# One sequence further ahead: where x is scaled, split and transposed in a mixture-of-experts MLP kernel

## What is computed

```python
h = gelu(einsum('bsh,bhi->bsi', x, Wi[expert]) + bi, approximate=False)   # 512 -> 2048
o = einsum('bsi,bih->bsh', h, Wo[expert]) + bo                            # 2048 -> 512
r = o + x
y = (r - mean(r)) * rsqrt(var(r) + 1e-12) * gamma + beta
out = rotate(y, theta, phi)    # pairs of features turned by two angles of the sequence
```

## Time and profile before

| | |
|---|---|
| time of the kernel before | 3029.11 us, median of 3 runs (3025.92 to 3030.88) |
| the profiled execution | 3023.2 us, its span from first to last instruction 3021.5 us |
| TensorE busy | 2744.7 us (91%) |
| VectorE busy | 2377.5 us (79%) |
| GpSimd busy | 1603.3 us (53%) |
| ScalarE busy | 887.4 us (29%) |

### The profile page before, as it was taken

One profiled execution on the slowest core, in us unless ns is written; L12 is line 12 of the kernel. 1 busy time (PEld: TensorE's weight loads), 2 busy tenths in 40 slices (PEclk: granted clock), 3 DMA queues, 4 the chain that ended last, 5 costly groups with the idle time before them and its releaser, 6 DMA issues.

```text
span 3021.5 us, 54615 instructions
## 1 busy us (share of the span) xinstructions
PE 2744.7 (91%) x12306; PEld 1220.8 (40%) x12307; DVE 2377.5 (79%) x5177; ACT 887.4 (29%) x1433; POOL 1603.3 (53%) x1619
## 2 busy tenths in 40 slices
PE   2888999889999989998999999999889989999998
PEld 1333444334444434433444444444334433444443
DVE  4688878877778887888877888878887788877777
ACT  4222332223332223322333222222223222233332
POOL 4879727973017974479700478706876479700000
PEclk9899999999999999999999999999999999999999
DMA  4546445655444655546544446545465546534343
GB/s 161 139 115 166 114 132 123 161 129 126 87 101 126 159 132 128 132 111 170 118 108 91 125 114 170 128 105 142 121 153 142 132 105 164 123 87 91 80 94 70
DMA packets 742560, 375.89 MB, mean 124 GB/s; under 512 B 682816, under 2 KB 682944, under 8 KB 733824
## 3 DMA queue, kind: packets, MB, share of 16 engines
q1 hardware_dynamic: 677568, 173.95, 29.9%
q0 software_dynamic: 25984, 130.29, 13.2%
q10 hardware_dynamic: 38976, 71.32, 7.3%
HBM read 174.13 MB, written 33.55 MB: 69 GB/s over the span
## 4 chain that ended last, share of the span: by engine, by line
PE 29%; DVE 29%; DMA 23%; issue 11%; DVEq 6%; ACTq 1%; POOL 1%; ACT 1%; SPq 0%; POOLq 0%
DMA xbuf<-in_x 16%; PE z_ps L825 15%; PE o_ps L841 14%; DVE h L638 7%; DMA hT<-h 5%; DVEq L195 3%; DVE xbuf L671 2%; DVE hid L627 2%; DVE x L632 2%; DVE ln L665 2%; DVE ln L667 2%; DVE xbuf L654 1%; DVE y L686 1%; DVE turned L683 1%; DMA xT<-x 1%
## 5 line engine op out<-in xcount | busy, mean ns | idle before, releaser
L825 PE MATMUL z_ps<-wi,xT 128*128 x6096 | 1449.0, 389 | 173.3 <-DMA xT<-x 119.5
L841 PE MATMUL o_ps<-wo,hT 128*128 x6144 | 1423.8, 382 | 47.7 <-DMA hT<-h 35.0
L825 PEld LDWEIGHTS z_ps<-wi,xT 128*128 128x128 f16 x6096 | 607.8, 100 | 945.7 <-issue 287.9
L841 PEld LDWEIGHTS o_ps<-wo,hT 128*128 128x128 f16 x6144 | 605.0, 98 | 791.0 <-issue 86.2
L471 ACT ACTIVATE hid<-hid 128x512 f32<-128x512 f32 x512 | 322.0, 629 | 1507.4 <-DVE hid L627 1506.2
L638 DVE SCALAR_TENSOR_TENSOR h<-hid,tok,h 128x512 f16<-128x512 f32 x512 | 494.4, 966 | 43.5 <-ACT h L479 31.0
L405 POOL TENSOR_TENSOR wi<-staged 128x512 f32<-128x512 f32 x112 | 133.8, 1195 | 650.1 <-DVE xbuf L648 639.1
L479 ACT ACTIVATE h<-hid,tok 128x512 f16<-128x512 f32 x512 | 369.6, 722 | 281.1 <-DMA hT<-h 262.0
L627 DVE SCALAR_TENSOR_TENSOR hid<-z_ps,tok,bi_all 128x512 f32<-128x512 f32 x512 | 382.2, 747 | 80.1 <-DVE y L686 28.1
L338 POOL TENSOR_SCALAR staged<-staged,wscale 128x512 f32<-128x512 f32 x224 | 197.7, 883 | 20.9
L646 DVE TENSOR_SCALAR ln<-inv,ex 128x1 f32 (+1 forms) x128 | 27.3, 214 | 211.5 <-issue 173.8
(11 more groups left out here) (124 smaller groups left out, 1771.3 us busy)
## 6 DMA issues: line engine op xcount, KB each, us to landing
staged<-in_L_cond_Wi POOLq DMA_DIRECT2D x56, 1024.0 KB, 5.7
staged<-in_L_cond_Wo POOLq DMA_DIRECT2D x56, 1024.0 KB, 6.1
xbuf<-in_x ACTq DMA_DIRECT2D x128, 256.0 KB, 2.7
out<-y ACTq DMA_DIRECT2D x128, 256.0 KB, 2.2
hT<-h SPq DMA_TRANSPOSE x512, 3.1
bi_all<-in_L_cond_bi POOLq DMA_DIRECT2D x7, 1024.0 KB, 7.5
wi<-in_L_cond_Wi SPq DMA_DIRECT2D x4, 1024.0 KB, 8.7
wo<-in_L_cond_Wo ACTq DMA_DIRECT2D x4, 1024.0 KB, 11.7
```

The source lines that it names most:

```text
L825: last = t.matmul(z_ps[:, n, :], xT16[:, j, a, k, :], wi16[:, bass.ds(b, 1), w, k, cs], start=(k == 0 and (a, w) == PASSES[0]), stop=(k == ...
L841: last = t.matmul(o_ps[:, j, :], hT16[:, n, a, c, :], wo16[:, bass.ds(b, 1), w, n * GC + c, :], start=(n == 0 and c == 0 and (a, w) == PAS ...
```

## The change

x is scaled and split one sequence further ahead. ScalarE, in iteration s, sums the squares of x(s+2) instead of x(s+1) and makes the high half of x(s+2) after the last `gelu_bank` instead of that of x(s+1) between banks 0 and 1; x is fetched three sequences ahead. The Gelu of bank 3 also waits for the transpose of x(s+1), since `x16` is overwritten next. VectorE makes the low half of x(s+1) at the head of the iteration, ahead of the residual, instead of after z bank 1, and the scale of x(s+2) after z bank 1 instead of that of x(s+1) after z bank 0. SyncE issues the transpose of x ahead of that of bank 3 of h. Before the loop, x(1) is summed, scaled and split among the boot work.

```diff
--- before.py
+++ after.py
@@ -257,10 +257,10 @@
                                        h16[:, n % HB].rearrange("p a t -> p (a t)")).then_inc(s_hT[n], 16)
 
             def iteration(s, k, inner=False):
+                if there(s, 1, inner):
+                    transpose_x(1 - k)
                 if there(s, -1, inner):
                     transpose_h(NB - 1)
-                if there(s, 1, inner):
-                    transpose_x(1 - k)
                 if there(s, 0, inner):
                     for n in range(NB - 1):
                         transpose_h(n)
@@ -465,8 +465,10 @@
                 act.sem_clear(s_sx)
                 a.activation(x16[:, 0, :], x_of(s), ACT.Copy, scale=SX).then_inc(s_xhi, 1)
 
-            def gelu_bank(s, k, n):
+            def gelu_bank(s, k, n, ahead):
                 hb = hid[:, n * BANK:(n + 1) * BANK]
+                if ahead and n == NB - 1:
+                    act.wait_ge(s_xT, (s + 2) * 16)
                 act.wait_ge(s_z, s * NB + n + 1)
                 a.activation(hb, hb, ACT.Gelu).then_inc(s_gelu, 1)
                 act.wait_ge(s_gelu, s * NB + n + 1)
@@ -484,18 +486,16 @@
                 act.dma_start(out[bass.ds(b, 1), :, :].rearrange("a t n -> t (a n)"), y[:]).then_inc(s_y, 16)
 
             def iteration(s, k, inner=False):
-                ahead, here = there(s, 1, inner), there(s, 0, inner)
-                if there(s, 2, inner):
-                    fetch_x(s + 2, k)
+                ahead, here = there(s, 2, inner), there(s, 0, inner)
+                if there(s, 3, inner):
+                    fetch_x(s + 3, 1 - k)
                 if ahead:
-                    sum_x(s + 1, 1 - k)
+                    sum_x(s + 2, k)
                 if here:
-                    gelu_bank(s, k, 0)
+                    for n in range(NB):
+                        gelu_bank(s, k, n, ahead)
                 if ahead:
-                    hi_x(s + 1)
-                if here:
-                    for n in range(1, NB):
-                        gelu_bank(s, k, n)
+                    hi_x(s + 2)
                 if there(s, -2, inner):
                     store(s - 2)
 
@@ -525,16 +525,20 @@
             e0 = slot_value(act, EXPERT, 0, E - 1)
             fetch_x(1, 1)
             sum_x(0, 0)
+            fetch_x(2, 0)
             squares(0, 1)
             hi_x(0)
             squares(0, 2)
             squares(0, 3)
+            sum_x(1, 1)
             for q in range(Q):
                 act.dma_start(by_rows(raws[1][:, q * QN:(q + 1) * QN]),
                               wo_quarter(e0, q)).then_inc(s_braw[Q + q], 16)
             act.wait_ge(s_ang, 1)
             a.activation(angle[:, 20:24], angle[:, 16:20], ACT.Sin).then_inc(s_sin, 1)
             hi_parts(0)
+            act.wait_ge(s_xT, 16)
+            hi_x(1)
             for q in range(Q):
                 squares(1, q)
             iteration(0, 0)
@@ -699,6 +703,8 @@
                     b, r = 0, 0
                 elif here:
                     b, r = slot_value(dve, BUF, s, 1), slot_value(dve, RANK, s, E - 1)
+                if ahead:
+                    lo_x(s + 1)
                 if last:
                     b2 = slot_value(dve, BUF, s - 2, 1)
                     residual(s - 2, k, b2)
@@ -709,8 +715,6 @@
                     moments(s - 2, b2)
                 if here:
                     z_bank(s, 0, b)
-                if ahead:
-                    scale_x(s + 1)
                 if back:
                     lo_group(s - 1, 1 - k, NB - 1)
                 if last:
@@ -718,8 +722,8 @@
                     normalise(s - 2, b2)
                 if here:
                     z_bank(s, 1, b)
-                if ahead:
-                    lo_x(s + 1)
+                if there(s, 2, inner):
+                    scale_x(s + 2)
                 if here:
                     lo_group(s, k, 0)
                 if last:
@@ -769,6 +773,7 @@
             v.tensor_scalar(angle[:, 16:18], r, -1.0, 1.5707963267948966, ALU.mult, ALU.add).then_inc(s_ang, 1)
 
             total(0)
+            scale_x(1)
```

## The result

The changed kernel takes 3132.52 us (median of 4 runs, 3131.84 to 3134.12) against 3027.52 us of the kernel before on the same chip (4 runs, 3025.89 to 3030.88): **105 us slower, ratio 1.0346, 95% interval 1.0328 to 1.0364.** The forecast was 3127 us.

What follows compares the result with a forecast made beforehand. The prediction took VectorE to bound most iterations. Its terms, 11 + 55 + 93 - 23 - 30 - 8 = +98 us on a profiled 3023.2 us, gave 3121; the runs' median is 5.9 us higher, hence 3127 us, range 3023 to 3190.

Steps and rivals of the forecast that it cites:

- VectorE sets the pace: Steady state: VectorE bounds 105 of 123 iterations, so removing TensorE's 119.5 us of waits gains nothing by itself.
- first stretch: Timeline from 725 to 894 us, GpSimd idle: eight iterations, 768 matmuls, 169 us, TensorE setting the pace.
- second stretch: Timeline from 1528 to 1697 us, GpSimd idle: eight iterations, 169 us, VectorE setting the pace.
- The low half of x at the head: VectorE's head: waits about 1 us for ScalarE's high half, with the third register load standing behind that wait.
- Rival 2: VectorE's head: the third load covers the low half if the high half ends 0.9 us sooner; 2937 us, chance 0.07.
- The stall in the quiet iteration: VectorE's head, GpSimd idle and VectorE pacing: 0.4 us in each of 27 iterations, +11 us.
- TensorE-paced iterations: 18 iterations where TensorE sets the pace: VectorE's 0.98 us wait for bank 3 covers the delay, 0 us.
- Late transposes: 19 iterations where bank 1's transpose of h lands late: the mean delay at VectorE's head is 4.9 us, +93 us.
- GpSimd busy: VectorE's head in 59 iterations with GpSimd working: mean delay 0.9 us, +55 us.
- Credits: VectorE's waits for TensorE shrink, -30 us; the middle of its list sheds a slowed low half, -8; boot 0.
- The scale of x behind z bank 1: VectorE's middle: its waits for the sum of x's squares go, -23 us.
- The transposes' new order: SyncE, x's transpose ahead of bank 3's of h: nothing queues behind it, no term in the sum.

Runs made afterwards that it cites:

- C: Changed kernel with only SyncE's transposes in the old order, bank 3 of h ahead of x: 3151.78 us, ratio 1.0414 to the kernel before.
- B: Changed kernel with low half of x back behind z bank 1 and transposes in the old order: 2967.90 us, ratio 0.9815 to the kernel before.
- A: Kernel before with only fetch, sum of squares and scale of x one sequence further ahead: 2964.87 us, ratio 0.9805.
- D: Changed kernel with the low half of x behind the moments, ahead of z bank 0: 2990.54 us, ratio 0.9891 to the kernel before.
- F: Changed kernel with the high half of x between bank 3's Gelu and its high half of h: 2942.79 us, ratio 0.9718 to the kernel before.
- J: Changed kernel with later experts' weight transfers cut to an eighth (wrong weights, timing only): 3094.96 us, ratio 1.0226 to the kernel before.
- I: Kernel before with later experts' weight transfers cut to an eighth (wrong weights, timing only): 3031.01 us, ratio 1.0010.
- G: Changed kernel with the high half of x made between banks 1 and 2 on ScalarE: 2909.16 us, ratio 0.9616 to the kernel before.
- K: G with VectorE's three register loads spread and the scales of h behind the moments: 2984.91 us, ratio 0.9861 to the kernel before.
- H: Changed kernel with three buffers of h instead of two: 3074.27 us, ratio 1.0148 to the kernel before.

## Why the prediction was right

The bound, the mechanism and the place were right. The time, 5.5 us from the one measured (+98 us in the sum, 109.7 in the span), was closer than the terms deserve, and that is luck. The prediction's terms for the low half at the head add up to 11 + 55 + 93 - 30 - 8 = +121 us, where C against B shows +181. It gave the scale of x -23, where A shows -59, and the order of the transposes nothing, where C shows -21. Sixty us too little on one side stand against 57 us of gain that it did not see on the other.

- *VectorE sets the pace, and the 119.5 us of TensorE's waits for x are worth nothing by themselves:* shown, as far as D can show it. They are gone in the changed kernel, which is slower, and in D, which gains less than A, where 82.5 us of them remain. The prediction's first stretch holds 773 matmuls and not 768; by VectorE's aggregations its quiet iterations took 20.9 us, those of the second stretch 21.1.
- *The low half of x at the head waits for the high half behind bank 3:* shown by C against B (+181 us) and by F (-190 us with the high half 1.8 us earlier). Rival 2's condition, 0.9 us sooner, pointed to the right place.
- *The stall in the quiet iteration,* +0.4 us: mis-sized, measured +0.16. The 21 quiet iterations that VectorE paced took 21.15 us, and the quiet ones take 21.31 now. Two durations were a little long. From the copy's end to that of the high half of x it is 0.62 us (the two overlap by 0.09), not 0.74, and from the low half to the residual 1.06, not 1.15. With the seam (0.14 for 0.17) the chain is 0.2 us shorter than worked out. Over all iterations the low half starts 1.07 us ahead of the residual in the median and 1.27 in the mean, since a load does not always take the 0.31 us that the prediction calls typical: of the 382 in the kernel before, 247 took under 0.35 us, the rest up to 1.04.
- *TensorE-paced iterations, 18 at 0:* mis-sized. The 11 quiet ones among them took 20.91 us and take 21.31 now, with VectorE pacing; for all 18 that would be about +7 us. With 4 instead of 11 us for the class above the two add up to what the prediction had.
- *Late transposes, 19 iterations and +93 us:* over-sized as a gross term. With bank 3's high half ending over 5.5 us behind bank 1's low half I counted 16, with 92 us of waiting at the low half in them, of which 36 are what 16 ordinary ones wait too: 56 us. In J the idle time ahead of the low half falls by 83 us. Together with what the kernel before lost to the same transfers elsewhere (the -23 of the sum's waits and the -30 of TensorE's stand for it in the prediction, net +40), I and J give a net 41.
- *GpSimd busy, +55 us:* not measured by itself. Of the 110 us, 8 belong to the quiet iterations and 41 to the transfers, so some 61 are left for it, a remainder that no run shows.
- *Credits:* VectorE's waits for TensorE fell by 45 us, not 30, and those for h's high half by 22, which the sum had left out. VectorE's instructions did not get 8 us cheaper (2432 and 2431 us behind the boot).
- *The scale of x behind z bank 1, -23:* the waits for the sum fall by 19 us in the changed kernel (23.0 to 3.9, the rest in the boot). But with the sum ahead, alone (A), it gives 59 us, which no step of the prediction saw. **Beside the size of the stall this was the largest effect that the prediction missed,** and of its 59 us only some 20 in idle time are explained.
- *The transposes' new order, nothing:* mis-sized; C shows that it gives some 20 us once the low half is at the head.

What stays open: VectorE's instructions take 2394 to 2500 us in sum, in kernels that differ only in the order of its list or not even in that. The durations go with what GpSimd does beside them, but no run here controls that, so differences of 40 us between variants are not to be read as the price of an edit by themselves. Of the step of 181 us, 30 are longer instructions of this kind (2403 to 2433 from B to C, in the profiled executions); the rest is idle time of VectorE.

## What to carry to other kernels

When a piece of work is moved ahead to spare one engine a wait, look at where its own input is made: the low half at the head cost 181 us because the high half had been put behind the last link of the longest chain between the two engines, and moving that one instruction up ScalarE's list turned a loss of 3.5% into a gain of 4%. Of two engines that are both nearly full, ask which one waits for less in sum, and count the register loads that no busy time holds; here 119 us of waits on the other one were worth nothing. And a bundle of edits can hide a good one: the first part alone gave 2%.

## What the runs showed of the hardware that was not expected

- The loads of a table entry into a VectorE register took 0.30 us at the least and often twice that: under 0.35 us in 247 of 382 in the kernel before, in 217 in G, in 79 in K and in 141 in H. They add up to 158 us in G, 231 in K and 225 in H. In K and H they are long above all while one of ScalarE's transfers (x in, output out) is under way: 0.70 us in the mean against 0.51 in K, 0.83 against 0.48 in H. No run tests that as the cause, and the place of the loads alone doesn't decide it, since H has them where the changed kernel has them (median 0.64 against 0.39).
- The transposing transfer of h lands in 3.0 us (median; 3.1 before). Where ScalarE had to wait long for one in the changed kernel, up to 8.3 us, a 1 MB weight transfer had been issued within 0.3 us of the end of the low half that the transpose carries, and landed first. With transfers an eighth as large the longest such wait was 2.3 us in J, but 5.6 in I.
- VectorE's instructions, the same in number and shape, took from 2394 to 2500 us in sum. A low half of h took 0.75 us with no GpSimd instruction beside it and up to 3.9 us with one.
